# Two of 32 row-maximum chunks moved to ScalarE and GpSimd, and the products with V of a unit issued together

## The reference

```
def attn_a(h, Wq, bq, Wk, bk, Wv, bv, Wo, bo):      # 32 heads of 8
    q, k, v = split(h @ Wq + bq), split(h @ Wk + bk), split(h @ Wv + bv)
    probs = softmax(einsum('bhqd,bhkd->bhqk', q, k) / sqrt(8))
    return merge(einsum('bhqk,bhkd->bhqd', probs, v)) @ Wo + bo
# attn_b: 8 key heads repeated to 32, and -1e10 added where i-128 <= j < i
def ffn(x):                                         # 256 -> 1024 -> 256
    h = silu(x @ w_gate) * (x @ w_up)
    return keep_2_largest_of_each_4(h) @ w_down
x = x + attn_a(ln(x)); x = x + ffn(ln(x)); x = x + attn_b(ln(x)); x = x + ffn(ln(x))
```

## Time and profile before

| | us |
|---|---|
| median of 3 runs | 1661.97 (1661.29 to 1664.39) |
| the profiled execution's own time | 1661.77 |
| its span, first to last instruction | 1659.8 |
| PE busy | 1609.1 (97%) |
| DVE busy | 1491.0 (90%) |
| ACT busy | 1281.8 (77%) |
| POOL busy | 266.8 (16%) |

### The profile page before, as it was taken

The page is one execution under the profiler, slowest core; times in us unless marked ns, Lnnn a source line. Parts: engine busy times, 40 slices in busy tenths (PEclk is TensorE's granted clock), DMA queues, the critical chain, the costliest instruction groups (busy, mean ns, idle before and its releaser), DMA issues.

```text
span 1659.8 us, 39596 instructions
## 1 busy us (share of the span) xinstructions
PE 1609.1 (97%) x14128; PEld 636.9 (38%) x14128; DVE 1491.0 (90%) x2168; ACT 1281.8 (77%) x2424; POOL 266.8 (16%) x623
## 2 busy tenths in 40 slices
PE   6899999999999999999988999999999999999999
PEld 3322222222222223787653222222222222237877
DVE  6999999999999997787678999999999999937765
ACT  3399999999999998433224999999999999983321
POOL 1410000000000000000012222333332233320000
PEclk9989999999999999999998999999999999999999
DMA  6943344334354321200404232222222322112000
GB/s 160 296 98 70 63 76 84 63 64 84 69 139 87 73 60 44 64 1 0 117 15 132 59 66 57 51 51 65 57 55 62 62 57 51 55 49 58 14 13 26
DMA packets 72126, 114.70 MB, mean 69 GB/s; under 512 B 12464, under 2 KB 27824, under 8 KB 71984
## 3 DMA queue, kind: packets, MB, share of 16 engines
q1 hardware_dynamic: 71984, 112.63, 29.2%
HBM read 71.96 MB, written 40.63 MB: 68 GB/s over the span
## 4 chain that ended last, share of the span: by engine, by line
PE 54%; DVE 35%; issue 7%; ACT 1%; DMA 1%; SPq 0%; DVEq 0%; POOLq 0%; ACTq 0%
DVE mneg L1306 28%; PE psum L785 18%; PE psum L767 11%; PE psum L737 7%; PE psum L887 5%; PE psum L843 5%; PE psum L848 2%; PE psum L700 2%; PE psum L823 2%; PE psum L720 1%; PE psum L682 1%; DVE area L1356 1%; DVE area L1390 1%; DVE stats L1199 1%; DVE area L1340 1%
## 5 line engine op out<-in xcount | busy, mean ns | idle before, releaser
L1055 ACT ACTIVATE area<-psum 128x512 f32<-128x512 f32 x2048 | 1097.2, 600 | 42.1 <-PE psum L767 13.7
L785 PE MATMUL psum<-area 128*32 128x256 f32 x8192 | 655.2, 392 | 0.4 <-POOL area L1568 0.4
L767 PE MATMUL psum<-area 51*128 51x512 bf16 x2048 | 639.2, 385 | 2.5 <-DVE vsb_b L1256 1.4
L1312 DVE CUSTOM_DVE_ANT_0 xn<-psum,band 128x1024 f32<-128x1024 f32 x512 | 588.4, 1220 | 10.3 <-PE psum L737 9.3
L1306 DVE TENSOR_REDUCE mneg<-psum 128x1 f32<-128x1024 f32 x512 | 581.0, 1211 | 7.0 <-PE psum L737 6.9
L785 PEld LDWEIGHTS psum<-area 128*32 128x32 f32 x8192 | 162.1, 108 | 400.7 <-issue 259.1
L737 PE MATMUL psum<-area 48*128 48x512 bf16 x1024 | 301.6, 385 | 8.2 <-DVE mneg L1306 5.1
L767 PEld LDWEIGHTS psum<-area 51*128 51x128 bf16 x2048 | 141.0, 94 | 427.0 <-ACT area L1055 353.3
L737 PE MATMUL psum<-k_max_b,area 48*128 48x512 bf16 x1024 | 292.8, 385 | 5.4 <-DVE mneg L1312 4.7
L1549 POOL TENSOR_TENSOR mparts<-mneg,nought 128x16 bf16<-128x16 f32 x64 | 14.1, 221 | 742.3 <-DVE mneg L1306 501.1
L1100 ACT ACTIVATE area<-psum 128x512 f32<-128x512 f32 x64 | 38.2, 599 | 115.9 <-PE psum L848 115.8
(11 more groups left out here) (89 smaller groups left out, 1092.1 us busy)
## 6 DMA issues: line engine op xcount, KB each, us to landing
ctx_rows<-area SPq DMA_DIRECT2D x64, 256.0 KB, 2.1
area<-q_stacks SPq DMA_DIRECT2D x32, 384.0 KB, 6.8
area<-k_stacks SPq DMA_DIRECT2D x64, 192.0 KB, 5.6
area<-q_stacks_b SPq DMA_DIRECT2D x32, 384.0 KB, 5.3
area<-q_stacks SPq DMA_DIRECT2D x32, 192.0 KB, 4.6
area<-q_stacks_b SPq DMA_DIRECT2D x32, 192.0 KB, 3.4
area<-ctx_rows SPq DMA_DIRECT2D x16, 256.0 KB, 4.1
area<-inv_rows SPq DMA_DIRECT2D x16, 256.0 KB, 4.5
```

Source lines behind the costliest of these rows:

```text
L767: pe.matmul(psum[:, BANK_OF["exp", g, u, head], :], k_st[lo:lo + ROWS + PARTS, buf, 0 if a else head // 2, kt * P:(kt + 1) * P], q_st[lo:l ...
L785: mm = pe.matmul(psum[head * VW:(head + 1) * VW, BANK_OF["ctx", g, qh], cols], vaug[:, buf, kt, head, :], probs[:, u % PRING, head, cols], ...
L1055: act.activation(probs[:, u % PRING, head, :], psum[:, BANK_OF["exp", like, u, head], :], ACT.Exp, scale=SCALE).then_inc(bank_freed, 1)
L1312: dve.tensor_tensor_reduce(band_out[:, c % 2, :], slot, band[:, at:at + SEQ], 1.0, -3.0e38, ALU.add, ALU.max, mneg[:, qh, col:col + 1]).th ...
```

## The change

In the first attention chunks 4 and 20 of every group but the first are no longer reduced by DVE from PSUM. ACT copies their 1024 columns to SBUF (`hold_scores`), between the exponentials of heads 1 and 2 of units 5 and 13; POOL folds them to 128 columns in nine instructions (`narrow_down`: maximum as subtract, clamp at zero, add); DVE reduces these 128 columns behind chunks 10 and 26 (`end_maximum`). PE's matmuls two chunks later wait for ACT's copy. In both attentions the two parts of the products with V stand together at the end of the unit. The bank list takes the ctx bank behind the fourth score block of a unit in place of the second.

```
+ON_ACT = (4, 20)
+ENDED_BEHIND = {10: 4, 26: 20}
@@ share_banks
-                if head == 1 and u % BT == LAG and (g or u >= BT):
+                if head == GH - 1 and u % BT == LAG and (g or u >= BT):
                     taken.append(("ctx", g, u // BT))
@@ max_scores
+                    if is_held(*divmod(G, GROUPS), old):
+                        pe.wait_ge(held, held_before(G, old) + 1)
+                    else:
+                        pe.wait_ge(max_used, maximum_at(*divmod(G, GROUPS), old) + 1)
@@ PE's group
-                        if u < LAG and first:
-                            scores(a, g, buf, u, 2 * step + 1, ahead)
-                        else:
-                            scores(a, g, buf, u, 2 * step + 1, ahead)
-                            times_v(*of, step, ahead or u < LAG)
+                        scores(a, g, buf, u, 2 * step + 1, ahead)
+                    if u >= LAG or not first:
+                        for part in range(2):
+                            times_v(*of, part, ahead or u < LAG)
@@ ACT
+            def hold_scores(g, c):
+                k = held_before(g, c)
+                act.wait_ge(max_ready, CHUNKS * g + c + 1)
+                if not isinstance(g, int) or k:
+                    act.wait_ge(narrowed, k)
+                bank = max_bank(0, g, c)
+                act.copy(hold[:], psum[:, bank:bank + 2, :].rearrange("p b c -> p (b c)")).then_inc(held, 1)
@@ exps, behind the exponential of a head
+                    c = LEAD + 2 * u + head // 2 - CHUNKS
+                    if a == 0 and ahead and head % 2 and c in ON_ACT:
+                        hold_scores(g + 1, c)
@@ DVE
+            def end_maximum(g, c):
+                qh, head, qt = chunk_of(c)
+                col = (head % 2) * (CPH // 2) + (head // 2) * (BT // HALF) + qt
+                dve.wait_ge(narrowed, held_before(g, c) + 1)
+                dve.tensor_reduce(mneg[:, qh, col:col + 1], narrow[:], AX.X, ALU.max, negate=True
+                                  ).then_inc(max_used, 1)
             def group(a, g):
                 for c in range(CHUNKS):
-                    maxima(a, g + 1, c)
+                    if not is_held(a, g + 1, c):
+                        maxima(a, g + 1, c)
+                    if a == 0 and c in ENDED_BEHIND:
+                        end_maximum(g + 1, ENDED_BEHIND[c])
@@ POOL
+            def narrow_down(g, c):
+                k = held_before(g, c)
+                pool.wait_ge(held, k + 1)
+                n = SEQ // 2
+                for i in range(3):
+                    near, far = hold[:, 0:n], hold[:, n:2 * n]
+                    s0 = 3 * k + i + 1
+                    pool.tensor_tensor(far, far, near, ALU.subtract).then_inc(held_less, 1)
+                    pool.wait_ge(held_less, s0)
+                    pool.sem_inc(above_started, 1)
+                    pool.tensor_scalar(far, far, 0.0, None, ALU.max).then_inc(held_above, 1)
+                    pool.wait_ge(held_above, s0)
+                    if i < 2:
+                        pool.tensor_tensor(near, near, far, ALU.add).then_inc(held_halved, 1)
+                        pool.wait_ge(held_halved, 2 * k + i + 1)
+                        n //= 2
...
+                pool.tensor_tensor(narrow[:], near, far, ALU.add).then_inc(narrowed, 1)
```

More of the change, by code:

```diff
@@ L79, in chunk_of, with is_held, maximum_at, held_before @@
     return qh, head, qt
+ON_ACT = (4, 20)
+ENDED_BEHIND = {10: 4, 26: 20}
+STEPS = []
+for _c in range(CHUNKS):
+    STEPS += ([] if _c in ON_ACT else [_c]) + ([ENDED_BEHIND[_c]] if _c in ENDED_BEHIND else [])
+NARROW = 128
+def is_held(a, g, c):
+    return a == 0 and c in ON_ACT and not (isinstance(g, int) and g == 0)
+def maximum_at(a, g, c):
+    return CHUNKS * (GROUPS * a + g) + (c if a or isinstance(g, int) and g == 0 else STEPS.index(c))
+def held_before(g, c):
+    return len(ON_ACT) * (g - 1) + ON_ACT.index(c)
 EVENTS = GH * UNITS + 2 * HALF
@@ L194, in hybrid_kernel @@
         wkv_b = [sb(f"wkv_b{i}", [P, DK, KV_HEADS * HD]) for i in range(2)]
+        wu_at = nc.sbuf_base
         wu_hi = sb("wu_hi", [P, DK, INNER // P, P], F32R)
@@ L211, in hybrid_kernel @@
         mT = sb("mT", [CPH * PARTS, HALF, P], BF16)
+        narrow = sb("narrow", [P, NARROW])
         sums_at = nc.sbuf_base
@@ L276, in hybrid_kernel, with over @@
                  + [parts_mid[:, i] for i in range(2)] + [parts_top[:, 0], parts_far[:, 0]])
-        def over(name, at, shape):
-            return nc.alloc_sbuf_tensor_at(name, shape, F32R, offset=at)
+        def over(name, at, shape, dt=F32R):
+            return nc.alloc_sbuf_tensor_at(name, shape, dt, offset=at)
         wg_hi = over("wg_hi", vsb_at, [P, DK, INNER // P, P])
@@ L289, in hybrid_kernel @@
         xd_lo = [over(f"xd_lo{c}", at, [P, DK, BANK]) for c, (_, at) in enumerate(xd_at)]
+        hold = over("hold", wu_at, [P, SEQ], F32)
         w_raw = [xnT[:, 2 * i:2 * i + 2].rearrange("p c k t -> p (c k t)").rearrange("p (k n) -> p k n", k=DK)
@@ L332, in hybrid_kernel @@
         mask_started, max_started = sem("mask_started"), sem("max_started")
+        above_started = sem("above_started")
+        held, held_less, held_above, held_halved, narrowed = (
+            sem(s) for s in ("held", "held_less", "held_above", "held_halved", "narrowed"))
         x_biased, x_attended, x_fed = sem("x_biased"), sem("x_attended"), sem("x_fed")
@@ L732, in max_scores @@
                         pe.wait_ge(rest_done, PBASE[1] + PCH[1])
-                if not isinstance(g, int) or n >= 2:
-                    pe.wait_ge(max_used, n if in_feed(a, g, c) else n - 1)
+                if in_feed(a, g, c):
+                    pe.wait_ge(max_used, n)
+                elif n >= 2:
+                    G, old = divmod(n - 2, CHUNKS)
+                    if is_held(*divmod(G, GROUPS), old):
+                        pe.wait_ge(held, held_before(G, old) + 1)
+                    else:
+                        pe.wait_ge(max_used, maximum_at(*divmod(G, GROUPS), old) + 1)
                 for half in (1, 0):
@@ L1235, in split_dense_weights @@
                 dve.wait_ge(vaug_ready, GROUPS)
+                dve.wait_ge(narrowed, len(ON_ACT) * (GROUPS - 1))
                 pairs = [(w_raw[i][:, k, :].rearrange("p (h c r) -> p h r c", h=2, r=4),
@@ L1308, in maxima @@
                     if not isinstance(g, int) or c >= 2 or g:
-                        dve.wait_ge(max_used, CHUNKS * G + c - 1)
+                        dve.wait_ge(max_used, maximum_at(a, g, c) - 1)
                     dve.sem_inc(max_started, 1)
@@ L1559, in split_max @@
                 pool.tensor_tensor(mparts[:, qh, :, 2, :], view(mres2), view(nought), ALU.add).then_inc(mparts_ready, 1)
+            def narrow_down(g, c):
[14 more added lines that the diff above has]
+                        n //= 2
+                if not isinstance(g, int) or k:
+                    first = c == ON_ACT[0]
+                    old = ON_ACT[ON_ACT.index(c) - 1]
+                    pool.wait_ge(max_used, CHUNKS * (g - first) + STEPS.index(old) + 1)
+                pool.tensor_tensor(narrow[:], near, far, ALU.add).then_inc(narrowed, 1)
             def mask_probs(a, g, u, ahead):
@@ L1584, in group @@
                         extend_v(a, g + 1, 1 - buf)
+                    for step in range(2):
+                        c = LEAD + 2 * u + step - CHUNKS
+                        if a == 0 and ahead and c in ON_ACT:
+                            narrow_down(g + 1, c)
             def make_band():
```

## The result

| | before | after |
|---|---|---|
| median, us | 1661.63 (4 runs) | 1832.03 (4 runs) |
| ratio | | 1.1024 (95%: 1.1005 to 1.1043) |
| span of the profiled execution | 1659.8 | 1831.0 |

The account below looks back on a forecast made before the run. DVE was taken to bound the kernel, PE 2% behind; after the change, a bank-wait chain of 2.39 us a unit. Sum 31.5+25.5-0.3+9.3+14.4 = +80.4 us on 1661.77, giving 1742; range 1708 to 1770.

Parts of the forecast that it names:

- Regrouping: Both attentions: 16 products together make a 2.39 us unit chain; +31.5 and +25.5, plus the last groups.
- last groups: Groups without chunks at each attention's end: longer chain and product blocks, +4.3 and +5.0 us.
- units 2 and 10: Fourth block takes the sums' bank; products wait for the exponential behind ACT's copy of the sums: 2.27 us each.
- bank wait: With three banks going round, a unit's fourth score block waits for the first's exponential; chain 2.39 us sets both attentions.
- DVE waits 0.13 a unit anyway: At 2.39 us a unit DVE has idle time, so its saved reductions gain nothing.
- Copies, +14.4: ACT's 30 copies in the first attention, 0.90 us each, delay the next unit by 0.48: +14.4 (10.8 to 16.8).
- DVE's saving is worth nothing: First attention: 30 reductions of 1.131 us spared on DVE gain no time; the short reduction hides in idle time.
- rival 1: DVE stays in front, chain under 2.26 us; moved chunks gain 0.37 x 30 = 11 us, 1651; chance 0.05.
- POOL fits by 0.4 us: POOL's fold of a moved chunk takes 6.5 us, with 6.9 before DVE reaches the short reduction.
- rival 4: POOL's fold is late: 0.5 us late gives 1751, 6 us late at twice the durations 1890; chance 0.08.

Follow-up runs that it names:

- v_only: Kernel before with only the regrouped products and their bank list, no chunk moved off DVE: 1740.15 us, ratio 1.0471.
- short_first: v_only with the first head's exponential halved to 256 columns in units 4 to 15: 1714.10 us, ratio 1.0328.
- short_fourth: v_only with the fourth head's exponential halved to 256 columns in units 4 to 15: 1739.58 us, ratio 1.0472.
- late_end: Changed kernel with the short reductions behind chunks 13 and 29 instead of 10 and 26: 1759.27 us, ratio 1.0577.
- hold_late: Changed kernel with products in their old order and short reductions moved behind chunks 13 and 29: 1673.88 us, ratio 1.0070.
- filled: Changed kernel with seven extra score matmuls in PE's pause before chunks 13 and 29: 1811.96 us, ratio 1.0913.
- fold_twice: Changed kernel with two folding rounds on POOL instead of three, DVE reducing 256 columns: 1762.07 us, ratio 1.0607.
- hold_only: Changed kernel with products back in their old order, so the moved chunks alone: 1808.81 us, ratio 1.0903.

## Why the prediction was wrong

- *Regrouping, forecast +66 us with the last groups.* Right in direction, 12 us too small: v_only has +78 (75 to 81), the group periods 38.69 and 38.80 against 38.3. Some 0.3 of the missing 0.4 to 0.5 a group is at units 2 and 10: the copy of the sums began 0.13 or 0.22 behind the first block, not 0.11, and such a unit took 2.37 or 2.45, not 2.27. That the bank wait holds the first attention is shown by short_first against short_fourth; that it alone is to blame is not: the second chain through DVE's two buffers, which I did not look for, is as long in the second attention. "DVE waits 0.13 a unit anyway" took DVE for independent.
- *Copies, +14.4.* Right: 0.48 each by the group periods (late_end less v_only, 0.96 a group).
- *DVE's saving is worth nothing.* Right in the regrouped order. In the old order (hold_late) it is eaten by ACT's copy; rival 1's 11 us never appeared.
- *POOL fits by 0.4 us.* This is the step that failed. It is the duration of the fold: 8.8 us for 6.5. The start (2.5 us into the unit; 479.25-476.76) and DVE's arrival (9.4; DVE began to wait at 488.12-1.83 = 486.29, 9.5 into it) were right, so instead of 0.4 us to spare there is a wait of 1.83. The one-input instruction was priced by another one-input instruction, 0.64 us for 512 columns; it takes 1.49, more than the two-input one, 1.27. Its three sizes took 2.85 where I had 1.3; the two-input ones, priced by a row that writes bfloat16, 4.9 for 4.5; and each clamp waits 0.2, not 0.08, for the instruction before it. I had this as rival 4, but gave it 8 in 100 and a price only at its near and its far end, 1751 and 1890; the range reached only to 1770.
- *What a late POOL costs* was mis-sized as well. Rival 4 let DVE pass on 0.3 of 0.5 us. With the clock kept (filled) the lateness costs (43.49-39.65)/2 = 1.92 us each time, twice a group: all of DVE's 1.83 reaches PE. The clock takes 1.3 a group more, so 5.2 a group, some 77 us in 15 groups; late_end and fold_twice give back 73 and 70 us. Neither the sum nor a rival had a term for the clock; in the earlier trace rows the last group kept 1.00 with a pause of 1.26 us.

By medians the runs give 170 us as 78 for the regrouping, 19 for the copies (1759.27-1740.15) and 73 for the late fold (1832.03-1759.27), 20 of these by the clock. By group periods it is 14 for the copies and 77 for the fold; the 5 us between the two accounts come mostly from late_end's longer stretch between the attentions.

## What to carry to other kernels

Count the buffers between two stretches of work that can't be interrupted: on three banks a run of four blocks made the consumer's latency part of the period in both places where it was put, and a saving on fixed costs of the producer is then paid with its own waiting. Offloading to a slow engine needs its latency priced from the same instruction and a reserve in the order, which cost nothing here (three chunks later: 73 us). And an in-order engine that stands in a pause may pay a second time in clock; filling the pause with useless work is a test for that.

## What the runs showed of the hardware

- POOL: clamp at zero (TENSOR_SCALAR, fp32 in place) 1.49, 0.84 and 0.52 us for 512, 256 and 128 columns of 128 partitions, TENSOR_TENSOR 1.27, 0.73 and 0.46; the affine select of 512 columns takes 0.64.
- TensorE's clock: behind 17 of 30 pauses of 1.8 to 2.0 us in one kernel, and 27 of 30 of 1.9 us in another (hold_only), the granted clock fell to 1.2 GHz, for 3 to 10 us of work almost without idle time; with the pause filled by seven matmuls it stayed at 2.4 GHz in the first attention, worth 20 us and 64 us.
- ACT's copy of 1024 columns from PSUM: 1.02 us listed, 0.89 to the next start; each of two of 512 is listed with 0.59 to 0.62.
